# Graph network kernel: part of layer one's plain edges read by wide one-hots instead of gathers, narrower tiles of sorted edges, pauses on VectorE, and a sum moved to TensorE

## The reference

```python
h = jnp.maximum(_layernorm(x, axis=-1), 0.0)
x = x + segment_sum((h * cj)[src], dst, 12500) * ci                  # layer one
h = jnp.maximum(_layernorm(x, axis=-1), 0.0)
x = x + h * (1 + eps[0]) + segment_sum(relu(h[src] + edge_attr), dst, 12500)  # layer two
```

## Time and profile before

| | us |
|---|---|
| median of 3 runs | 6152.03 (6150.35 to 6169.10) |
| the profiled execution, its time | 6146.08 |
| its span, first to last instruction | 6144.3 |
| GpSimd busy | 4655.4 |
| VectorE busy | 3122.4 |
| TensorE busy | 2601.4 |
| ScalarE busy | 1243.8 |
| mean granted TensorE clock | 0.671 |

### The profile page before, as it was taken

How to read it: one execution, slowest core, us unless ns; L and a number is a source line. 1 busy time by engine, 2 the same in 40 slices (tenths; PEclk the granted TensorE clock), 3 DMA queues, 4 the chain that set the end, 5 groups by cost and what they waited for, 6 DMA issues and landing times.

```text
span 6144.3 us, 89788 instructions
## 1 busy us (share of the span) xinstructions
PE 2601.4 (42%) x32958; PEld 2184.0 (36%) x32958; DVE 3122.4 (51%) x8199; ACT 1243.8 (20%) x2303; POOL 4655.4 (76%) x4404
## 2 busy tenths in 40 slices
PE   0322333333222223333332322234577887787776
PEld 0312222222222112222222211123466676666665
DVE  6534444433443334444333433223787777877776
ACT  0201111111111001111111110011333333333332
POOL 5777777777777777777777777776677777777774
PEclk9756666666665556666666655566678777878887
DMA  4311222222222211222222222102111121111211
GB/s 83 75 34 27 46 46 46 46 46 46 45 46 46 46 27 34 46 46 46 47 46 45 45 46 45 26 16 55 37 49 47 48 60 47 50 47 47 60 47 25
DMA packets 442929, 278.32 MB, mean 45 GB/s; under 512 B 341686, under 2 KB 411686, under 8 KB 436086
## 3 DMA queue, kind: packets, MB, share of 16 engines
q1 hardware_dynamic: 300926, 183.48, 12.4%
q0 software_dynamic: 140000, 83.16, 7.9%
q10 hardware_dynamic: 1560, 5.60, 0.3%
HBM read 192.42 MB, written 79.52 MB: 44 GB/s over the span
## 4 chain that ended last, share of the span: by engine, by line
POOL 73%; issue 22%; DVE 3%; DMA 1%; PE 0%; SPq 0%; ACT 0%; POOLq 0%; DVEq 0%; ACTq 0%
POOL records L552 32%; POOL message L542 21%; POOL stage L542 20%; DVE arena L1132 1%; PE plain_ps L855 0%; DMA stage<-table,src_plain 0%; DMA xs<-in_x 0%; DMA stage<-in_edge_attr 0%; DVE arena L1120 0%; SPq L402 0%; DVE arena L1308 0%; DVE centered L1156 0%; DVE counts L1014 0%; DMA table<-centered 0%; DMA record<-records 0%
## 5 line engine op out<-in xcount | busy, mean ns | idle before, releaser
L552 POOL DMA_INDIRECT records<-stage,place_i x1875 | 1939.1, 1034 | 605.4 <-issue 571.4
L542 POOL DMA_INDIRECT stage<-table,src_plain x1250 | 1368.6, 1095 | 404.4 <-issue 379.1
L542 POOL DMA_INDIRECT message<-table,src_plain x1250 | 1320.0, 1056 | 380.9 <-issue 380.9
L1120 DVE TENSOR_SCALAR arena<-arena,row_key 125x1280 bf16<-125x1280 f16 x1000 | 525.3, 565 | 1731.9 <-ACT arena L657 1731.9
L801 PE MATMUL key_rows<-ident,record 128*125 128x128 f16 x5000 | 461.5, 250 | 1734.2 <-DMA record<-records 1660.0
L1132 DVE TENSOR_SCALAR arena<-window_iota,dst_rel 128x320 bf16<-128x320 f16 x5000 | 1167.7, 305 | 3.6
L801 PEld LDWEIGHTS key_rows<-ident,record 128*125 128x125 f16 x5000 | 424.3, 163 | 1773.3 <-issue 1350.7
L657 ACT ACTIVATE arena<-key_rows 125x640 f16<-125x640 f16 x1000 | 647.5, 703 | 1727.2 <-PE key_rows L801 1720.8
L838 PE MATMUL sorted_agg<-arena 128*96 128x320 bf16 x5000 | 924.7, 341 | 102.4 <-DVE arena L1132 101.1
L855 PE MATMUL plain_ps<-centered,message 128*96 128x128 bf16 x2500 | 577.1, 402 | 466.8 <-DMA message<-table,src_plain 457.5
L838 PEld LDWEIGHTS sorted_agg<-arena 128*96 128x96 bf16 x5000 | 661.5, 141 | 239.9 <-DVE arena L1132 136.8
(11 more groups left out here) (122 smaller groups left out, 2024.4 us busy)
## 6 DMA issues: line engine op xcount, KB each, us to landing
record<-records SPq DMA_DIRECT2D x50, 1650.0 KB, 7.4
stage<-in_edge_attr SPq DMA_DIRECT2D x125, 400.0 KB
records<-pad SPq DMA_DIRECT2D x25, 1650.0 KB
records<-stage,place_i POOLq DMA_INDIRECT x1875, 2.1
message<-table,src_plain POOLq DMA_INDIRECT x1250, 2.4
stage<-table,src_plain POOLq DMA_INDIRECT x1250
table<-parts ACTq DMA_DIRECT2D x4, 585.9 KB
xs<-in_x SPq DMA_DIRECT2D x4, 390.6 KB
```

Of the source, the lines that this page charges most:

```text
L542: pool.indirect_dma_start(message[:, k, j, :] if l == 0 else rows[:, k, j, :], None, table0 if l == 0 else table1, bass.IndirectOffsetOnAx ...
L552: pool.indirect_dma_start(records, bass.IndirectOffsetOnAxis(ap=place_i[:, h, e:e + 1], axis=0), stage[:, h, e, :], None).then_inc(scatter ...
L1120: nc.vector.tensor_scalar(src_onehot[:, g % 2, o, :], key_row[:, g % 2, :], row_key[0:NP, o:o + 1], None, ALU.is_equal).then_inc(src_oneho ...
```

## The change

**Layer one, direct tiles.** Of each plain unit's 25 tiles the first DIRECT = 10 are no longer gathered, in all batches but the last: 20 of a batch's 50. Their sources' features are picked from `parts` in SBUF. Their keys are loaded and split once at the start (9 small VectorE instructions over all batches, and 2 per plain unit for the destinations). Per batch there are 20 tiles in 5 sub-steps of SUB = 4. For each sub-step TensorE turns 4 keys, ScalarE copies them, VectorE builds WIDES = 20 one-hots of source of 512 columns. For each tile TensorE makes WIDES = 20 products of 480 moving columns (MEMBERS = 5 table columns at once, 96 each), ScalarE copies the 480 columns, VectorE builds one one-hot of 640 columns for member and destination, and TensorE makes 5 products of 128 columns into the same sum as the gathered tiles.

**Other parts.** `record` has one half in layer one; the other half and `xs` hold wide one-hots, so x is loaded again at the layer's end. The padding pattern has 10 tiles in place of 20. GpSimd scatters batch b and then gathers b's 30 tiles. Ranks are made two batches ahead, amid the wide part. Rank is counted from the middle of a bucket, so the first tile of a bucket holds lower destinations and the second higher ones; a tile then has a window of WT = 224 columns instead of 320 (first tile 0 to 223, second 96 to 319; the first product of a batch keeps 320). The plain one-hots are 128-column instructions, one per tile, contiguous. VectorE waits for its own last instruction (a pause) after every 3 destination one-hots in layer one and 5 in layer two, after every 5 plain ones, after each source one-hot, after every 2 wide ones, each member one-hot, and each large instruction of the ranks; each scan is cut in two. In layer two TensorE adds the attributes with one f32 product (identity, 320 columns) per group and `add_attr` goes. At the start the destinations of batch 0 and the units' first destinations are loaded ahead, the smallest destination is no longer searched for, and the first batch is ranked before x is looked at.

```diff
+    WT = 224
+    UP = WA - WT
-    PAD = 20
+    PAD = 10
+    DIRECT = 10
+    MEMBERS = 5
+    WIDES = C // MEMBERS
+    SUB = 4
...
             def step0(b, h, u):
-
-                if is_first(b):
-                    scatter(b, h, u)
-                if left_after(b) >= 1:
-                    scatter(b + 1, 1 - h, u + h)
+                scatter(b, h, u)
                 pool.wait_ge(src_plain_loaded[h], 16 * u)
...
-                    gather(0, k, gathered[0][k], src_plain[:, h, k * J:(k + 1) * J])
+                    gather(0, k, gathered_tiles(b), gathered[0][k], src_plain[:, h, k * J:(k + 1) * J])
...
+                def pick_wide(b, n):
+                    s, i = n // SUB, n % SUB
+                    if n < 2:
+                        pe.wait_ge(message_ready[0], 2 * GROUPS * (b + 1))
+                    else:
+                        pe.wait_ge(wide_copied, DIRECTS * b + n - 1)
+                    for w in range(WIDES):
+                        if i == 0 and w % PAIR == 0:
+                            pe.wait_ge(wide_ready, PAIRS * (SUBS * b + s) + w // PAIR + 1)
+                        last = nc.tensor.matmul(candidates[n % 2][:, 0:MEMBERS * WIDE], wide_onehot[s % 2][w][:, i * P:(i + 1) * P],
+                                                parts[:, w * MEMBERS:(w + 1) * MEMBERS, :].rearrange("p c w -> p (c w)"),
+                                                start=(w == 0), stop=(w == WIDES - 1))
+                    last.then_inc(wide_picked, 1)
...
-                        at_least(pe, sum_ready, nth - 1)
+                        at_least(pe, left_ready, nth - 1)
+                        nc.tensor.matmul(candidates[g % 2][:, 0:GROUP * F], ident[:], record[:, h, g * GROUP:(g + 1) * GROUP, 0:F],
+                                         start=True, stop=False)
...
+                    run = 5 if l == 1 else 3
                     for t in range(GROUP):
                         tile = g * GROUP + t
-                        last = nc.vector.tensor_scalar(dst_onehot[:, g % 2, t, :], window_iota[:], dst_rel[:, h, tile:tile + 1],
+                        last = nc.vector.tensor_scalar(dst_onehot(g, t), window_iota[:, 0:WA if tile == 0 else WT], dst_rel[:, h, tile:tile + 1],
                                                        None, ALU.is_equal)
+                        if t % run == run - 1 and t < GROUP - 1:
+                            last.then_inc(dst_paused[l], 1)
+                            dve.wait_ge(dst_paused[l], nth * ((GROUP - 1) // run) + t // run + 1)
...
+                    for w in range(WIDES):
+                        one = nc.vector.tensor_scalar(wide_onehot[s % 2][w], direct_row[:, s % 2, :], wide_key[:, w:w + 1], None, ALU.is_equal)
+                        if w % PAIR == PAIR - 1:
+                            one.then_inc(wide_ready, 1)
+                            dve.wait_ge(wide_ready, PAIRS * (SUBS * b + s) + w // PAIR + 1)
+                    for i in range(SUB):
+                        n = s * SUB + i
+
+                        at_least(dve, direct_done, DIRECTS * b + n - 3)
+                        nc.vector.tensor_scalar(member_onehot[:, n % DB, :], window_iota[:], direct_dst[:, n // DIRECT, bass.ds(b, 1), n % DIRECT],
+                                                None, ALU.is_equal).then_inc(member_ready, 1)
+                        dve.wait_ge(member_ready, DIRECTS * b + n + 1)
...
-                    if not is_first(b):
+                    if is_last(b):
                         for k in range(PLAIN):
-                            plain_onehots(b - 1, k)
+                            plain_onehots(b, k)
+                        add_sorted(b)
+                    else:
+                        wide_onehots(b, 0)
+                        wide_onehots(b, 1)
                         for k in range(PLAIN):
-                            add_plain(b - 1, k)
-                    add_sorted(b)
+                            plain_onehots(b, k)
+                        add_sorted(b)
+                        wide_onehots(b, 2)
+                        if left_after(b) >= 2:
+                            rank_within(b + 2, h, u + 1)
+                        for s in range(3, SUBS):
+                            wide_onehots(b, s)
+                        if left_after(b) >= 2:
+                            rank_all(b + 2, h, u + 1)
+                    for k in range(PLAIN):
+                        add_plain(b, k)
```

More of the change, by code:

```diff
@@ new lines, in direct_products @@
+                def direct_products(b, n):
+                    k, j = n // DIRECT, n % DIRECT
+                    pe.wait_ge(wide_copied, DIRECTS * b + n + 1)
+                    pe.wait_ge(member_ready, DIRECTS * b + n + 1)
+                    if j == 0:
+                        plain_bank_free(b, k)
+                    for m in range(MEMBERS):
+                        last = nc.tensor.matmul(plain_agg[k], direct_message[n % DB][:, m * WIDE:(m + 1) * WIDE],
+                                                member_onehot[:, n % DB, m * WS:(m + 1) * WS], start=(j == 0 and m == 0), stop=False)
+                    last.then_inc(direct_done, 1)
+                    if j == DIRECT - 1:
+                        plain_products(b, k)
@@ L878, in group @@
                             turn_keys(*ahead(l, b, h, u, g + 3))
+                        if g in (7, 8) and not is_last(b):
+                            turn_direct_keys(b, g - 7)
                         if g >= 0:
@@ L1153, in third_part, with window_onehots @@
                                             ALU.subtract).then_inc(message_ready[1], 1)
-                def window_onehots(k, keys):
-                    return nc.vector.tensor_tensor(plain_onehot[:, k, :, :], plain_iota[:],
-                                                   keys.unsqueeze(1).to_broadcast([P, WS, J]), ALU.is_equal)
+                def window_onehots(k, keys, tiles, pauses):
+                    for j in tiles:
+                        last = nc.vector.tensor_scalar(plain_onehot[:, k, j, :], window_iota[:, 0:WS], keys[:, j:j + 1], None, ALU.is_equal)
+                        if pauses is not None and j % 5 == 4 and j < J - 1:
+                            last.then_inc(plain_paused[l], 1)
+                            dve.wait_ge(plain_paused[l], pauses + (j - tiles[0]) // 5 + 1)
+                    return last
```

423 lines of the change are left out of this document (275 added, 148 removed).

## The result

| | before | after |
|---|---|---|
| median, us | 6159.94 (6150.35 to 6169.1, 4 runs) | 5391.04 (5389.12 to 5396.81, 4 runs) |
| profiled execution, its span | 6146.1, 6144.3 | 5396.81, 5395.0 |

The ratio is 0.8753, with a 95% interval of 0.8735 to 0.8772: 12.5% faster.

A forecast was written before the change was run, and what follows sets the result against it. GpSimd's indirect DMAs were taken to bound the kernel. Start 43 + first scatter 101 + record landing 8 + 24 batches 3456 + last gathers 65 = 3673; seam 61, layer two 1687, tail 59: span 5480, median 5490 us; range 5310 to 5770.

The forecast's parts named there:

- the first rival: Layer one's wide part: TensorE's clock drops for part of it, 10 to 25 us per batch lost, say 5850 us; chance 0.13.
- Start: Before layer one's first scatter: batch 0's rank needs its sources alone, first scatter at 43 us, 20 us gained.
- Wide part: Layer one's direct tiles: TensorE 4.5 us per tile, 90 us for 20, at 2.4 GHz; VectorE's five sub-steps 42 us.
- fifth rivals: Layer one: wide products set everything, slower than before from 172 us per batch, 0.28 us per product; chance 0.08.
- The third: Both layers: pauses do nothing, wide one-hots disturb GpSimd like the rest; 15 and 7.5 us per batch, 5696 us; chance 0.12.
- The chain: Layer one, VectorE and TensorE: 39 us to groups done plus 102 us to the end of `rank_all`, 141 us per batch.
- Interference in layer one: GpSimd's DMAs lengthened by other engines: 8 us per batch (4 to 15), down from 11.5, so GpSimd needs 140 us.
- Interference in layer two: GpSimd's gathers lengthened by other engines: from 7.5 to perhaps 5 us per batch, layer two 1687 us, 62 less.
- The fourth rival: Both layers: GpSimd's interference nearly goes, 1 to 2 us per batch; layer two 63.5 per batch, 5320 us; chance 0.10.
- Layer two's engines: Layer two, per batch: VectorE +1 us in all, TensorE between -9 and +3 us, both hidden under GpSimd's 50 gathers.
- The second rival: Layer two is held by VectorE and TensorE in turn, so the 62 us don't come: 5550 us; chance 0.12.
- Waits: Layer one: gathers wait for the previous batch's products; second set of 15 free, only the last batch's 50 wait for both.

The follow-up runs named there:

- the last run: Changed kernel with layer two's 25 indirect gathers per plain unit replaced by one ordinary 400 KB transfer, on the second chip: 7992.8 us, ratio 0.9628.

## Why the prediction was right, point by point

Its steps held in kind nearly everywhere. In the span it was 85 us too slow (5480 for 5395.0), and these are mostly one term; of the other 14 us of the 99, 12 lie between profiled execution and median, which was 5.9 us above before and is 5.8 us below after, and 2 in rounding up. Two of its sums are off: at 25 us per batch the first rival comes to 6090, not 6000, and both of the forecast's lower bounds together to 5260, not 5310. Neither decided anything.

- **Start**: 40.5 for 43 us; tail 53 for 59, seam 58 for 61. 11 of the 85 us.
- **Wide part**: its products go at 0.203 us each (20 from 2958.80 to 2962.85) where I had 0.21 by a line through 320 columns, a tile at 4.33 for 4.5, the clock at 0.97 to 1.00. The wait at tile 12 was 1.07 + 2.2 = 3.3 us for "about 4", the sub-step of 20 one-hots 6.45 for 6.7 us. TensorE was done, with the products that follow the last tile, 98.6 us after the part began; on VectorE `rank_all` started at 83.3 for "near 83" and ended at 101.7 for "near 102". The first and fifth rivals fell with that: no clock drop and no 0.28 us product. The third fell with the interference below.
- **The chain**: 143.3 us per batch for 141. A group takes VectorE 3.78 us; two pauses in the sources and three in the targets bring the mean of a narrow one-hot to 303 ns, no less than a wide one had without. The ten groups are 38.2 us on VectorE, near the 39 I counted from the record's landing. What I left out is the hand-over behind `rank_all`, the two sums and the first keys of the next batch: 2 and 5 us in turn. I had them at nothing.
- **Interference in layer one**: scatters at 1005 ns and gathers at 993, each with 0.305 us to the next, are 5.2 us per batch over the undisturbed DMA, where I had 8. So GpSimd needs 75 x 1.310 + 30 x 1.298 = 137.2 us and waits 5.7. I had both bounds at 140 and 141 and 3 us of rubbing; the one was 3 us less and the other 2 more, and that 144 came so near is partly luck, since the rubbing stood where the hand-over was missing. The wide part's pauses and the halved scans had no run of their own, so what each of them gave is not shown. Record loads 142.7 us apart for 144 are 31 us over 24 batches, of which layer one's ends took 11 back (3609.8 for 3630): 20 of the 85 us.
- **Interference in layer two**: the term that was mis-sized. "Perhaps 5" was 2.8 us per batch (1002 ns + 0.30, against the 1.25 of an undisturbed gather), and layer two took 1633.5 us for 1687: 53 of the 85 us. The run without pauses shows its source: with them gone it is 8.7. The fourth rival had layer two at 63.5 us per batch, the forecast at 67.5; 65.3 lies half-way.
- **Layer two's engines**: I said that VectorE's and TensorE's changes there are hidden. TensorE's are: plain products take 0.06 us each (25 in 1.56) as forecast, and the old strided ones showed only through VectorE's instruction. VectorE's are not: half of what the sum of attributes would add to a batch comes through. The second rival, VectorE and TensorE in turn, fell as stated, since without gathers they need 58.8 us (an estimate from another chip), 6.5 below GpSimd's 65.3.
- **Waits**: that the second set of gathers is "free" was nearly so, 5.7 us per batch, because the chain and not GpSimd binds, by about that much.

The Trainium skill (SBUF — State Buffer, the sections SBUF: two separate sides and Who interferes with whom) says that VectorE in a two-port mode holds the port pair it shares with GpSimd for the whole instruction, so that GpSimd can't write descriptors meanwhile. The runs on the first kind of chip agree in direction: 1119 ns per gather without pauses, 1002 with, 950 undisturbed. A lock held for one instruction would last 0.6 us at most in the groups, and a wait of VectorE for itself behind it would let GpSimd in, which fits; that it is this lock was not shown by a run of its own.

My prediction counted the 3.65 us gather as agreeing with that rule. It is no case of it: the instructions beside it are `TENSOR_TENSOR`. In Who interferes with whom the Trainium skill (SBUF — State Buffer) gives `tensor_tensor` no two-port mode and has it contend, with both inputs in SBUF, with GpSimd's reads alone. That such an instruction holds a gather up is what the trace shows (3.65 us beside two of 1.84 us each, 0.94 undisturbed); by which port, no run tells.

The Trainium skill's remedy (SBUF — State Buffer, the section SBUF: two separate sides) is a DMA issued from ScalarE's or SyncE's queue, whose descriptors GpSimd does not make. No run here tried it: the ordinary transfers of the last run still went out from GpSimd's queue, 50 issues of 0.575 us. They gained 1559 us on a chip where the sufferers were the other engines and GpSimd's DMAs were undisturbed at 957 ns, which the rule on the shared ports doesn't describe.

## What to carry to other kernels

When one engine's instructions are taken away because it binds, put the time that the others then need beside it in full, groups and new part together, and say how far apart the two bounds are: here 143.3 and 137.2 us, so a further gain on the chain alone is worth 6 us per batch at most, and one on GpSimd alone nothing. Where GpSimd issues indirect DMAs beside back-to-back one-hots on VectorE, short waits of VectorE for itself can be worth more than they cost (146 us in layer two), but only where GpSimd binds or would bind without them. Time such a trade on more than one chip: work moved from indirect DMAs to many small instructions on TensorE and VectorE gained 12.5% on one kind of chip and lost 15% on another.

## What the runs showed of the hardware that was not expected

- On two chips TensorE, VectorE and ScalarE did hardly any instructions while GpSimd issued indirect DMAs: 36 products in 90 us against 578, many of them single ones at steps of 0.7 us or multiples of it. With 1,250 gathers turned into 50 ordinary transfers, layer two went from 120.7 to 58.8 us per batch.
- The time of one undisturbed 128-row indirect DMA on GpSimd was the same on all chips, 0.94 to 0.96 us and 0.30 to the next.
- A scan of 625 elements takes 1.46 us, one of 1,250 2.75; cut in halves, with a wait after each, they let scatters through at 1.1 to 1.4 us instead of 2.43.
